# Self-attention followed by a pooled non-local block: the matrix engine's work spread evenly, the DMAs' partial row sums merged by the vector engine, and a new order of loads where the second layer starts

## The chip, the cores and the metric

The kernel runs on one core of a Trainium2 chip. The metric is the device time of one execution in microseconds (us), as a median over runs. The engines are called by the names of the profile: PE is the matrix engine (PEld its weight loads), ACT the scalar engine, DVE the vector engine, POOL the general-purpose engine, which issues one of the two DMA queues, and SP the engine that only issues DMAs. Sixteen DMA engines carry the transfers of both queues.

## The reference, cut to what matters

`x` is 2 x 256 x 64 x 64 in float32, so each of two batches has 256 channels at n = 4096 places. Layer 0 is self-attention with 8 heads of 32 channels; layer 1 is a non-local block with 1024 pooled keys.

```python
# layer 0
qkv = einsum('oc,bchw->bohw', w_qkv, x); q, k, v = split(qkv, 3)      # 8 heads, d = 32
attn = softmax(einsum('bhdi,bhdj->bhij', q, k) / sqrt(d), axis=-1)    # 4096 x 4096 for each head
out = einsum('bhij,bhdj->bhdi', attn, v)
x = einsum('oc,bchw->bohw', w_proj, out.reshape(b, c, h, w)) + x
# layer 1
theta = conv1x1(x[:, :64]); phi = maxpool2(conv1x1(x[:, 64:])); g = maxpool2(conv1x1(x))
y = softmax(theta^T phi, axis=-1) @ g
x = batchnorm(conv1x1(y)) + x
```

## The kernel before

**Stages.** Each batch passes through five stages: projection and attention of head group 0 (four heads), projection and attention of head group 1, and the second layer. The attention stages are most of the time. Each engine has one program, written out by hand in the order in which it is to work, and waits on semaphores.

**One attention stage.** The queries are cut into NC = 8 chunks of CH = 512, the keys into JT = 32 tiles of 128. One key tile of one chunk has four heads, which makes four "units" of 128 keys x 512 queries. ACT turns three units at a time into exponentials (line 595), from one of two PSUM banks of three units, into a ring of 36 units (nine key tiles) in SBUF. Such a group of three is a "step"; a stage has 342 steps, a chunk has 42 2/3. At step k PE waits for the exponentials of step k, computes the scores of step k + 2 (line 513, 12 matmuls in float16) and then some of the product with the values (`values`, line 526, float32). The product is counted in "halves": four matmuls, one for each head, on 256 of the 512 queries of a key tile. `halves_by(k)` says how many halves are done by the end of step k: 1.5 on average, at most two behind what is ready.

**Row sums.** The softmax's denominators are sums over keys. The key tiles of a chunk are added up elementwise: those in `SUM_V` by DVE into `acc` (line 648), those in `SUM_D` (eight) by POOL's accumulating DMAs into `accD`, two DMAs for each tile (k = 0, 1; lines 674 and 677), each waiting for the one before it of its own k. Then PE multiplies with a matrix of ones: `sums_of_acc` (line 489) five steps into the next chunk, `sums_of_dma` (line 497) nine steps into it. DVE copies the chunk's output out of PSUM (`output_out`, line 605) in the middle of the chunk's last add, which it splits in two for that, and the sums (`sums_out`, line 613) before the add of key tile 11 of the next chunk; the reciprocal (line 651) follows the add of tile 21. The last chunk of a stage is summed after the stage (`tensor_end`, lines 485 to 497).

**Slots.** Before ACT writes a key tile into the ring, `slot_free` waits until the tile nine before it has been used: by the values, and by DVE's add or by both accumulating DMAs.

**From attention to the second layer.** Unnormalised outputs went to DRAM (`o_dram`), inverse sums too (`r_dram`). When the last scores are out, SP issues (`rows_ahead`, line 1296) the projection's weights, the outputs of chunks 1 to 3 (`output_in`, line 1288) and then the inverse sums of chunks 0 to 6 as rows (line 1303). PE spreads the rows over the partitions with a small matmul (`broadcast`, line 838) for chunks 0, 1, 2 and 7; for chunks 3 to 6 (`BY_DMA`) SP's DMAs do it (`spread_rows`, line 1239, two DMAs of 256 KB each). DVE multiplies (`normalise`, line 1092), PE projects (line 848). In `sync` SP issues all eight spreading DMAs, then the outputs of chunks 4 to 7, then stores the last chunk's inverse sums (line 1260), waits for that to land, and loads them as rows (line 1247), which `broadcast(7)` needs.

Of the kernel before, what the change touches and what calls it, by code (L numbers as in the profile page):

```python
# [18 lines left out]
G = 4  # L19
# [22 lines left out]
SUM_D = [2, 6, 9, 13, 16, 20, 23, 27]  # L42
# [21 lines left out]
def halves_by(k):  # L64

    if k == GROUPS - 1:
        return 2 * NC * JT
    halves = min(k * GROUP // 2, 2 * (min((k + 1) * GROUP, UNITS) // G))
    return halves - (halves % (2 * JT) in (1, 2 * JT - 1))
# [20 lines left out]
def conv_seq(nc, x, wqkv, wproj, gw, tw, pw, ww, vectors, biases, out, r_dram, r1_dram):  # L90
# [3 lines left out]
    with ExitStack() as root:  # L94
# [351 lines left out]
        def attention(g, ready_for, ahead):  # L446
# [7 lines left out]
            s_sum = sem(root, f"s_sum_{g}")  # L454
            s_o_free = sem(root, f"s_o_free_{g}")
# [22 lines left out]
            def sums_of_acc(pe, c):  # L478
                if c < NC - 1:
                    pe.wait_ge(s_o_free, c + 1)  # L480
                else:
                    pe.wait_ge(s_l_free, c)
                    r = (NC * JT - 1) * G % RING
                    for h in range(G):
                        nc.tensor.matmul(sums_in(c)[h * D:(h + 1) * D, :], ones[:], P[:, r + h, :],
                                         start=True, stop=False)
                pe.wait_ge(s_add, adds_by(c))
# [5 lines left out]
            def sums_of_dma(pe, c):  # L493
                for k in range(2):
                    pe.wait_ge(s_dma[k], 16 * len(SUM_D) * (c + 1))
                for h in range(G):
                    last = nc.tensor.matmul(sums_in(c)[h * D:(h + 1) * D, :], ones[:], accD[c % 2][:, h, :],
                                            start=False, stop=True)
                last.then_inc(s_sum, 1)

            def tensor(pe, free):
# [38 lines left out]
                for k in range(GROUPS):  # L540
# [25 lines left out]
            def tensor_end(pe):  # L566
                sums_of_acc(pe, NC - 1)
                sums_of_dma(pe, NC - 1)
# [37 lines left out]

            def sums_out(dve, c):
                dve.wait_ge(s_sum, (c + 1) * 2)
                if c:
                    dve.wait_ge(s_out, 16 * c)  # L610
                elif ahead:
                    dve.wait_ge(ahead.signals["out"], 16 * NC)
                nc.vector.tensor_copy(L[:], sums_in(c)).then_inc(s_l_free, 1)

            def vector(dve, at, room):
# [9 lines left out]
                for c in range(NC):  # L625
                    for n in range(ADDS):
                        if n == 7 and c:
                            sums_out(dve, c - 1)
# [13 lines left out]
                        if j == JT - 1:  # L642
                            nc.vector.tensor_tensor(new[:, 0:2, :], old[:, 0:2, :], P[:, r:r + 2, :], ALU.add)
                            output_out(dve, c)
                            nc.vector.tensor_tensor(new[:, 2:G, :], old[:, 2:G, :], P[:, r + 2:r + G, :], ALU.add
                                                    ).then_inc(s_add, 1)
                        else:
                            nc.vector.tensor_tensor(new, old, P[:, r:r + G, :], ALU.add).then_inc(s_add, 1)  # L648
                        if n == 14 and c:
                            dve.wait_ge(s_out, 16 * c)  # L650
                            nc.vector.reciprocal(Ls[:, g, c - 1:c, :], Ls[:, g, c - 1:c, :]).then_inc(s_inv, 1)
# [4 lines left out]
            def gpsimd(pool, clean):  # L656
                for c in range(NC):
# [3 lines left out]
                    for i, j in enumerate(SUM_D):  # L661
                        for k in range(2):
# [4 lines left out]
                            if i == 0:  # L667
                                if c:
                                    pool.wait_ge(s_dma[k], 16 * len(SUM_D) * c)
                                if c >= 2:  # L670
                                    pool.wait_ge(s_sum, (c - 1) * 2)
                                elif ahead:
                                    pool.wait_ge(ahead.signals["sum"], (NC - 1 + c) * 2)
# [30 lines left out]
            sems = [s_ready, s_exp, s_pv, s_add, s_sum, s_o_free, s_l_free, s_out, s_inv, s_r, s_b, s_tr, s_ost] + s_dma + s_q  # L704
# [3 lines left out]
        def second_layer(behind, homes):  # L708
# [98 lines left out]
            def gpsimd(pool, b, clean):  # L807
                if b is not None:
                    pool.wait_ge(behind.signals["sum"], NC * 2)
# [432 lines left out]
            def sync(sp, b, dram, following):  # L1242
# [388 lines left out]
```

## Time and profile before

| | |
|---|---|
| median of 3 runs | 2556.77 us (2555.61 to 2557.37) |
| the profiled execution | 2555.43 us, of which the span of its instructions is 2553.8 us |
| PE busy | 2461.8 us (96%) |
| ACT busy | 2220.2 us (87%) |
| DVE busy | 2144.3 us (84%) |
| POOL's DMA queue, share of the 16 DMA engines' time | 52.7% |

The profile is one execution, its times counted from the first instruction. A busy share is an average over stages with different limits, and matmuls are pipelined, so that PE is shown busy where it isn't at its peak; idle time before an instruction, and what ended it, tells more. The attention stages are at about 44 to 514, 552 to 1023, 1310 to 1780 and 1816 to 2287 us.

### The profile page before, as it was taken

The page shows a single profiled execution, that of the slowest core. Times are in us where ns is not written, and L with a number is a line of the kernel's source. Part 1 is how long each engine was busy: PE and PEld are TensorE (multiplying, and loading weights), DVE is VectorE, ACT ScalarE, POOL GpSimd, SP SyncE. Part 2 cuts the span into 40 slices and gives each one's busy share as a digit, 9 for nine tenths or more (in the row PEclk, how much of TensorE's full clock was granted, in tenths as well). Part 3 has the DMA queues.
Part 4 walks back from the last instruction along what each step waited for, and adds up shares of the span by engine and source line. Part 5 has one row for each costly group of instructions (what it writes and reads, how often), then busy time and mean ns, then how long its engine had stood idle before and what let it go on. Part 6 is the DMA issues. An engine that isn't in the chain of part 4 may idle for free.

```text
span 2553.8 us, 74568 instructions
## 1 busy us (share of the span) xinstructions
PE 2461.8 (96%) x33252; PEld 1076.2 (42%) x33256; DVE 2144.3 (84%) x1382; ACT 2220.2 (87%) x1826; POOL 455.7 (18%) x652
## 2 busy tenths in 40 slices
PE   8999999999999999699999999999999999987998
PEld 4444444444444444244454444444444444433443
DVE  6999999979999999596579999998799999976954
ACT  7999999989999999266489999998999999983663
POOL 0222222202222222010002222222122222220100
PEclk9999999999999999899999999999999999998999
DMA  8777777767777777401277787776777777682011
GB/s 240 161 156 154 160 156 159 151 177 160 158 155 155 159 160 155 114 1 71 82 200 160 157 161 155 157 148 142 198 157 156 160 156 158 144 176 71 1 58 43
DMA packets 150227, 360.14 MB, mean 141 GB/s; under 512 B 23072, under 2 KB 65376, under 8 KB 149632
## 3 DMA queue, kind: packets, MB, share of 16 engines
q0 software_dynamic: 73728, 268.47, 52.7%
q1 hardware_dynamic: 76176, 86.92, 11.2%
q8 instruction: 258, 4.23, 0.7%
q14 instruction: 65, 0.53, 0.1%
HBM read 52.76 MB, written 33.85 MB: 34 GB/s over the span
## 4 chain that ended last, share of the span: by engine, by line
PE 34%; ACT 29%; issue 16%; DMA 13%; DVE 6%; SPq 1%; ACTq 0%; POOL 0%; POOLq 0%; DVEq 0%
ACT arena L595 27%; DMA arena<-arena 11%; PE scores L513 8%; PE psOL L526 7%; PE psOL L952 6%; DVE arena L648 3%; PE scores L334 3%; PE psOL L875 1%; DMA arena<-att_out 1%; PE scores L345 1%; SPq L1239 1%; PE scores L939 1%; PE scores L940 1%; PE scores L929 1%; PE scores L930 1%
## 5 line engine op out<-in xcount | busy, mean ns | idle before, releaser
L595 ACT ACTIVATE arena<-scores 128x1536 f32<-128x1536 f32 x1368 | 1847.8, 1534 | 33.3 <-PE scores L513 29.9
L648 DVE TENSOR_TENSOR arena<-arena 128x2048 f32<-128x2048 f32 x704 | 1613.2, 2292 | 141.1 <-ACT arena L595 89.3
L513 PE MATMUL scores<-arena 96*32 96x512 f16 x16384 | 1128.1, 380 | 11.7 <-ACT arena L595 10.7
L526 PE MATMUL psOL<-arena 128*32 128x256 f32 (+1 forms) x13312 | 1117.1, 428 | 1.3 <-ACT arena L595 1.3
L513 PEld LDWEIGHTS scores<-arena 96*32 96x32 f16 x16384 | 382.5, 95 | 702.8 <-ACT arena L595 404.7
L677 POOL DMA_DIRECT2D arena<-arena x448 | 388.0, 895 | 1150.8 <-ACT arena L595 911.7
L526 PEld LDWEIGHTS psOL<-arena 128*32 128x32 f32 x13312 | 399.3, 110 | 370.7 <-issue 43.3
L952 PE MATMUL psOL<-arena 128*128 128x512 f16 x768 | 170.3, 379 | 0.0
L674 POOL DMA_DIRECT2D arena<-arena x64 | 35.2, 554 | 570.6 <-ACT arena L595 570.3
L1216 DVE SCALAR_TENSOR_TENSOR arena<-arena 128x1536 f16<-128x1536 f32 (+1 forms) x48 | 75.9, 1581 | 65.1 <-ACT arena L1062 63.3
L1055 ACT ACTIVATE arena<-scores 128x1536 f32<-128x1536 f32 (+1 forms) x48 | 62.5, 1301 | 72.0 <-PE scores L940 72.0
L952 PEld LDWEIGHTS psOL<-arena 128*128 128x128 f16 x768 | 75.1, 98 | 90.6
L992 ACT ACTIVATE arena<-X 128x512 f16<-128x512 f32 x32 | 20.2, 630 | 105.7 <-DVE X L1098 105.7
L1034 ACT ACTIVATE arena<-scores,arena 128x1024 f32<-128x1024 f32 x64 | 71.1, 1112 | 26.9 <-POOL arena L819 25.6
L334 PE MATMUL scores<-arena,wq_hi 128*128 128x512 f16 x256 | 72.3, 385 | 10.5 <-DVE wq_lo L263 8.6
L1202 DVE TENSOR_REDUCE arena<-scores 128x1 f32<-128x1024 f32 x64 | 78.0, 1221 | 5.0 <-PE scores L930 3.0
L376 ACT ACTIVATE arena<-scores 128x1024 f16<-128x1024 f32 x32 | 32.7, 1021 | 40.9 <-PE scores L334 40.0
L1062 ACT ACTIVATE arena<-arena 128x1536 f16<-128x1536 f32 (+1 forms) x48 | 64.4, 1341 | 2.8
L397 DVE SCALAR_TENSOR_TENSOR arena<-X,arena 128x1024 f16<-128x1024 f32 x32 | 39.1, 1223 | 27.8 <-ACT arena L363 27.8
L848 PE MATMUL scores<-arena 128*128 128x512 f32 x128 | 61.1, 622 | 0.0
L939 PE MATMUL scores<-arena 128*128 (+1 forms) x128 | 48.5, 379 | 6.1 <-ACT arena L1055 5.7
L929 PE MATMUL scores<-arena 128*128 128x512 f16 x128 | 48.7, 381 | 5.5 <-ACT arena L1034 5.4
(120 smaller groups left out, 1240.7 us busy)
## 6 DMA issues: line engine op xcount, KB each, us to landing
arena<-arena POOLq DMA_DIRECT2D x512, 512.0 KB, 5.3
arena<-qk_parts SPq DMA_DIRECT2D x192, 128.0 KB, 3.8
qk_parts<-arena SPq DMA_DIRECT2D x32, 512.0 KB, 3.7
X<-in_x SPq DMA_DIRECT2D x16, 512.0 KB, 5.1
att_out<-arena SPq DMA_DIRECT2D x32, 256.0 KB, 2.1
arena<-att_out SPq DMA_DIRECT2D x16, 512.0 KB, 12.2
out<-arena SPq DMA_DIRECT2D x32, 256.0 KB, 2.0
arena<-att_inv SPq DMA_DIRECT2D x16, 256.0 KB
```

Of the source, the lines that this page charges most:

```text
L334: last = nc.tensor.matmul(slot(w), wq[wp][:, t, outs], xp[:, t, c * CH:(c + 1) * CH], start=(n == 0 and t == 0), stop=(n == 2 and t == CT ...
L513: last = nc.tensor.matmul(bank[k % 2][m * D:(m + 1) * D, i * CH:(i + 1) * CH], KS[0:3 * D, h, j * 128 + m * D:j * 128 + (m + 1) * D], QS2[ ...
L526: last = nc.tensor.matmul(both(c)[h * D:(h + 1) * D, lo:hi], V[:, j, h * D:(h + 1) * D], P[:, r + h, lo:hi], start=(j == 0), stop=(j == JT ...
L595: nc.scalar.activation(P[:, u % RING:u % RING + size, :], bank[k % 2][:, 0:size * CH].rearrange("p (u n) -> p u n", n=CH), ACT.Exp, scale= ...
L648: nc.vector.tensor_tensor(new, old, P[:, r:r + G, :], ALU.add).then_inc(s_add, 1)
L677: nc.gpsimd.dma_start(dst, src, accum_op=ALU.add).then_inc(s_dma[k], 16)
L929: nc.tensor.matmul(two_banks(i)[:, ks], TA[:, its], PA[:, ks], start=True, stop=False)
L939: nc.tensor.matmul(dst, PA[:, m], TA[:, bass.ds(c * CH, CH)], start=True, stop=False)
L952: last = nc.tensor.matmul(psOL[:, t * CH:(t + 1) * CH], w[:, m, ts], v[:, p, m, :], start=(n == 0), stop=(n == 3 * MT - 1))
L1034: nc.scalar.activation(junk[:, i % 2, :], two_banks(i), ACT.Exp, bias=stat[:, 0, i:i + 1], scale=SCORE1, accum_out=l1[:, i:i + 1]).then_in ...
L1202: nc.vector.tensor_reduce(mx[:, i:i + 1], two_banks(i), AX.X, ALU.max).then_inc(s_mx, 1)
L1216: nc.vector.scalar_tensor_tensor(out=Pl[:, p, ms, :], in0=P32[:, p, ms, :], scalar=PS, in1=Ph[:, p, ms, :], op0=ALU.mult, op1=ALU.subtract ...
```

## The change

Five things are changed.

1. `SUM_D` has nine key tiles, mostly three apart, and `SUM_V` 23 instead of 24.
2. DVE adds `accD` to `acc` itself (`merge`), before its add of key tile 10 of the next chunk; PE has one product with ones for each chunk (`sums_of_both`), 18 steps into the next chunk, instead of two. The last chunk of a stage is summed as before.
3. `halves_by_step` replaces `halves_by`: halves are done at an even rate of 68 x 3 / 128 = 1.594 a step, start at step 6, and pause for four halves at the step with the product with ones. They trail what is ready by up to eight halves at the start and six or seven later.
4. DVE's last add of a chunk isn't split any more; `output_out` comes before its add of key tile 3 of the next chunk, `sums_out` before that of tile 19, the reciprocal after that of tile 25.
5. `rows_ahead` loads the rows of inverse sums first, then the weights and the outputs of chunks 1 and 2 only. In `sync` each chunk's two spreading DMAs are followed by that chunk's output (chunks 3 to 6), and chunk 7's output comes last.

```diff
-SUM_D = [2, 6, 9, 13, 16, 20, 23, 27]
+SUM_D = [2, 5, 8, 12, 15, 18, 21, 24, 27]
...
-    halves = min(k * GROUP // 2, 2 * (min((k + 1) * GROUP, UNITS) // G))
-    return halves - (halves % (2 * JT) in (1, 2 * JT - 1))
+SUMS, BEHIND = 18, 2
+SUM_STEPS = [exps_through(c, JT - 1) + SUMS for c in range(NC - 1)]
+def halves_by_step():
+    rate = (2 * JT + 4) * GROUP / (G * JT)
+    first = exps_through(0, JT - 1) + SUMS
+    start = first - (first * GROUP / 2 - BEHIND) / rate
+    done, at = [], 0
+    for k in range(GROUPS):
+        ready = 2 * (min((k + 1) * GROUP, UNITS) // G)
+        share = int(rate * (k + 1 - start)) - 4 * sum(1 for n in SUM_STEPS if n <= k)
+        to = ready if k == GROUPS - 1 else min(ready, share)
+        to -= to % (2 * JT) in (1, 2 * JT - 1)
+        at = max(at, to)
+        done.append(at)
+    return done
...
-            def sums_of_acc(pe, c):
+            def sums_of_both(pe, c):
+                pe.wait_ge(s_o_free, c + 1)
+                pe.wait_ge(s_merged, c + 1)
                 for h in range(G):
-                    last = nc.tensor.matmul(sums_in(c)[h * D:(h + 1) * D, :], ones[:], acc[c % 2][:, h, :],
-                                            start=(c < NC - 1), stop=False)
+                    last = nc.tensor.matmul(both(c)[h * D:(h + 1) * D, :], ones[:], acc[c % 2][:, h, :],
+                                            start=True, stop=True)
                 last.then_inc(s_sum, 1)
...
                     for c in range(NC - 1):
-                        if k == exps_through(c, JT - 1) + 5:
-                            sums_of_acc(pe, c)
-                        if k == exps_through(c, JT - 1) + 9:
-                            sums_of_dma(pe, c)
-                    at, end = halves_by(k - 1) if k else 0, halves_by(k)
+                        if k == exps_through(c, JT - 1) + SUMS:
+                            sums_of_both(pe, c)
+                    at, end = HALVES[k - 1] if k else 0, HALVES[k]
...
+            def merge(dve, c):
+                for k in range(2):
+                    dve.wait_ge(s_dma[k], 16 * len(SUM_D) * (c + 1))
+                dve.wait_ge(s_add, adds_by(c))
+                nc.vector.tensor_tensor(acc[c % 2], acc[c % 2], accD[c % 2], ALU.add).then_inc(s_merged, 1)
...
-                        if n == 7 and c:
+                        if n == 1 and c:
+                            output_out(dve, c - 1)
+                        if n == 6 and c:
+                            merge(dve, c - 1)
+                        if n == 12 and c:
                             sums_out(dve, c - 1)
...
                                 if c >= 2:
-                                    pool.wait_ge(s_sum, (c - 1) * 2)
+                                    pool.wait_ge(s_merged, c - 1)
...
                 for n in BUFFERS:
                     spread_rows(sp, dram, n)
+                    c = BY_DMA[n]
+                    if c >= 4:
+                        sp.wait_ge(s_oin[c % 4], 16)
+                    output_in(sp, c)
                 if b is not None:
                     sp.wait_ge(behind.signals["ost"], 16 * NC)
-                for c in range(4, NC):
-                    sp.wait_ge(s_oin[c % 4], 16)
-                    output_in(sp, c)
+                sp.wait_ge(s_oin[(NC - 1) % 4], 16)
+                output_in(sp, NC - 1)
...
             def rows_ahead(sp, dram):
-                sp.dma_start(wp_sb, wproj.rearrange("(t p) o -> p t o", p=128)).then_inc(s_wp, 16)
-                for c in range(1, 4):
-                    output_in(sp, c)
                 for k in range(2):
                     cs = slice(ROWS[k] * CH, ROWS[k + 1] * CH)
                     for g in range(NG):
                         sp.dma_start(Rr[32 * g:32 * g + G, cs], r_dram[dram, g * G:(g + 1) * G, cs]).then_inc(s_rc[k], 16)
+                sp.dma_start(wp_sb, wproj.rearrange("(t p) o -> p t o", p=128)).then_inc(s_wp, 16)
+                for c in range(1, 3):
+                    output_in(sp, c)
```

## Rows read from the trace of the kernel before

**Rows 1.** lines of instructions, costliest first: busy, mean ns of one | idle before them and what ended it

```profile
L595 ACT ACTIVATE arena<-scores 128x1536 f32<-128x1536 f32 x1368 | 1847.8, 1534 | 33.3 <-PE scores L513 29.9
L648 DVE TENSOR_TENSOR arena<-arena 128x2048 f32<-128x2048 f32 x704 | 1613.2, 2292 | 141.1 <-ACT arena L595 89.3 <-DVE arena L648 1.4
```

**Rows 2.** ACT in order of time, two stretches between its idle times: start, length, what

```profile
114.13 5.48 ACT L595 ACTIVATE arena<-scores 128x1536 f32<-128x1536 f32 x4 [0.62 <-PE scores L513]
120.22 52.69 ACT L595 ACTIVATE arena<-scores 128x1536 f32<-128x1536 f32 x39 [0.62 <-PE scores L513]
```

**Rows 3.** who waited for whom over the whole span: total us, times, longest

```profile
ACT arena L595 <- PE scores L513: 29.9, 68, 0.6
...
POOL arena L677 <- DMA arena<-arena: 237.2, 117, 5.6
...
DVE arena L1092 <- DMA arena<-att_out: 25.3, 2, 12.7
...
PE scores L838 <- DMA arena<-att_inv: 15.8, 2, 8.4
```

**Rows 4.** PE in order of time around one product with ones, 170 to 173 us

```profile
170.50 0.82 PE L513 MATMUL scores<-arena 96*32 96x512 f16 x12
171.15 1.04 PE L489 MATMUL psOL<-arena,ones 128*32 128x512 f32 x8
172.01 0.61 PE L526 MATMUL psOL<-arena 128*32 128x256 f32 x8
172.44 0.83 PE L513 MATMUL scores<-arena 96*32 96x512 f16 x12
```

**Rows 5.** PE in order of time: a stage's end, and two `broadcast` of the second layer

```profile
513.95 1.92 PE L526 MATMUL psOL<-arena 128*32 128x512 f32 x16 [0.34 <-ACT arena L595]
...
1031.78 2.08 PE L838 MATMUL scores<-arena,spread 4*128 4x512 f32 x4 [7.36 <-DMA arena<-att_inv]
...
1085.97 1.13 PE L838 MATMUL psOL<-arena,spread 4*128 4x512 f32 x4
```

**Rows 6.** DMAs of 60 to 500 us: share of 16 engines' time; issues, KB each, us to landing

```profile
q0 software_dynamic: 17442, 63.52, 72.7%
...
arena<-arena POOLq DMA_DIRECT2D x121, 512.0 KB, 5.3
...
att_out<-arena SPq DMA_DIRECT2D x7, 256.0 KB, 2.1
```

**Rows 7.** POOL in order of time: two issues of one chain (k = 1)

```profile
190.17 0.86 POOL L677 DMA_DIRECT2D arena<-arena  x1 [1.31 <-DMA arena<-arena]
...
197.16 0.87 POOL L677 DMA_DIRECT2D arena<-arena  x1 [2.92 <-ACT arena L595]
```

**Rows 8.** one piece of the chain that ended last, at the second layer's start

```profile
1054.31 16.30 DMA arena<-att_out
```

**Rows 9.** SP's DMA issues in order of time, second layer's start

```profile
1021.77 0.39 SPq L1297 DMA_DIRECT2D arena<-in_w_proj  x1
...
1040.75 13.12 SPq L1239 DMA_DIRECT2D arena<-att_inv  x8
...
1062.85 5.77 SPq L1260 DMA_DIRECT2D att_inv<-Ls  x2
1075.38 0.63 SPq L1247 DMA_DIRECT2D arena<-att_inv  x2
```

**Rows 10.** DVE in order of time: `normalise` of chunk 3, and of chunk 4

```profile
1052.44 1.21 DVE L1092 TENSOR_TENSOR arena<-arena 128x1024 f32<-128x1024 f32 x1
...
1070.63 1.23 DVE L1092 TENSOR_TENSOR arena<-arena 128x1024 f32<-128x1024 f32 x1 [12.70 <-DMA arena<-att_out]
```

**Rows 11.** windows: us, length, busy of the engines, granted clock, DMA share, GB/s

```profile
1042.00:1056.00 14.00, 14.00 (x41) 5.72 (x40) 10.78 (x17) 4.92 (x8) 0.70 (x1) 1.00 0.26 89
1058.00:1066.00 8.00, 1.22 (x3) 0.19 (x1) 0.00 (x0) 0.83 (x2) 0.00 (x0) 0.88 1.04 239
1066.00:1074.00 8.00, 1.48 (x4) 0.58 (x5) 3.27 (x5) 0.63 (x1) 0.00 (x0) 0.50 0.30 99
```

More of the change, by code:

```diff
@@ L61, in adds_through @@
     return max(1, sum(1 for t in SUM_V if t <= j) - 1)
-def halves_by(k):
-    if k == GROUPS - 1:
-        return 2 * NC * JT
-    halves = min(k * GROUP // 2, 2 * (min((k + 1) * GROUP, UNITS) // G))
-    return halves - (halves % (2 * JT) in (1, 2 * JT - 1))
+SUMS, BEHIND = 18, 2
[13 more added lines that the diff above has]
+    return done
+HALVES = halves_by_step()
 BY_DMA = [3, 4, 5, 6]
@@ L454, in attention @@
             s_sum = sem(root, f"s_sum_{g}")
+            s_merged = sem(root, f"s_merged_{g}")
             s_o_free = sem(root, f"s_o_free_{g}")
@@ L476, in adds_by, with sums_of_last @@
                 return (c + 1) * ADDS - (c == NC - 1)
-            def sums_of_acc(pe, c):
[L479 to L487, printed above, removed]
+            def sums_of_both(pe, c):
+                pe.wait_ge(s_o_free, c + 1)
+                pe.wait_ge(s_merged, c + 1)
                 for h in range(G):
-                    last = nc.tensor.matmul(sums_in(c)[h * D:(h + 1) * D, :], ones[:], acc[c % 2][:, h, :],
-                                            start=(c < NC - 1), stop=False)
+                    last = nc.tensor.matmul(both(c)[h * D:(h + 1) * D, :], ones[:], acc[c % 2][:, h, :],
+                                            start=True, stop=True)
                 last.then_inc(s_sum, 1)
-            def sums_of_dma(pe, c):
+            def sums_of_last(pe):
+                pe.wait_ge(s_l_free, NC - 1)
+                r = (NC * JT - 1) * G % RING
+                for h in range(G):
+                    nc.tensor.matmul(psO[h * D:(h + 1) * D, :], ones[:], P[:, r + h, :], start=True, stop=False)
+                pe.wait_ge(s_add, adds_by(NC - 1))
+                for h in range(G):
+                    nc.tensor.matmul(psO[h * D:(h + 1) * D, :], ones[:], acc[(NC - 1) % 2][:, h, :],
+                                     start=False, stop=False)
                 for k in range(2):
-                    pe.wait_ge(s_dma[k], 16 * len(SUM_D) * (c + 1))
+                    pe.wait_ge(s_dma[k], 16 * len(SUM_D) * NC)
                 for h in range(G):
-                    last = nc.tensor.matmul(sums_in(c)[h * D:(h + 1) * D, :], ones[:], accD[c % 2][:, h, :],
+                    last = nc.tensor.matmul(psO[h * D:(h + 1) * D, :], ones[:], accD[(NC - 1) % 2][:, h, :],
                                             start=False, stop=True)
@@ L566, in tensor_end @@
             def tensor_end(pe):
-                sums_of_acc(pe, NC - 1)
-                sums_of_dma(pe, NC - 1)
+                sums_of_last(pe)
             def slot_free(act, m):
@@ L641, in vector @@
                             old = new
[L642 to L649, printed above, removed]
+                        nc.vector.tensor_tensor(new, old, P[:, r:r + G, :], ALU.add).then_inc(s_add, 1)
+                        if n == 16 and c:
                             dve.wait_ge(s_out, 16 * c)
@@ L670, in gpsimd @@
                                 if c >= 2:
-                                    pool.wait_ge(s_sum, (c - 1) * 2)
+                                    pool.wait_ge(s_merged, c - 1)
                                 elif ahead:
-                                    pool.wait_ge(ahead.signals["sum"], (NC - 1 + c) * 2)
+                                    pool.wait_ge(ahead.signals["sum"], NC - 1 + c)
                                 nc.gpsimd.dma_start(dst, src).then_inc(s_dma[k], 16)
@@ L808, in gpsimd @@
                 if b is not None:
-                    pool.wait_ge(behind.signals["sum"], NC * 2)
+                    pool.wait_ge(behind.signals["sum"], NC)
                 nc.gpsimd.memset(TB[CM:128, :].bitcast(F32), 0.0).then_inc(s_pad, 1)
```

4 lines of the change are left out of this document (2 added, 2 removed).

## The prediction

> **What bounds the kernel now.** I read the lines by cost first. ACT's exponentials keep it busy for 1847.8 us and it stands idle before them for only 33.3 us, 29.9 of it for PE's scores [rows 1, 3]. 39 of them take 52.69 us, so a step takes ACT 1.351 us [rows 2], and 342 steps of four stages 1848 us. That is a floor the change doesn't touch. So the attention stages can give at most those 33 us. Then PE in order of time. Where it never waits for ACT, the scores of a step take 0.65 us (170.50 to 171.15), one product with ones 0.86 (to 172.01), one half 0.43 (to 172.44); two halves are four matmuls of the product's shape, so 0.86 [rows 4]. A step costs PE 0.65 + 1.5 x 0.43 = 1.30 us on average, 0.05 less than ACT's. A chunk has 42.7 steps and so 2.2 us to spare, of which the two products take 1.7. PE may fall behind by the 0.70 us that the scores leave of a step before ACT waits; a product in a step of two halves makes 0.65 + 3 x 0.43 + 0.43 = 2.37 us, 1.02 behind at once, and four steps later only 0.2 has been made good when the second product comes. That is the pair of 0.62 us waits in rows 2, 68 waits in all [rows 3]. Last the waits of the rest: at the start of the second layer PE waits 15.8 us in two batches for the rows of inverse sums and DVE 25.3 us for an output from DRAM [rows 3].
>
> **PE in the attention stages.** One product with ones fewer a chunk saves 0.86 us of PE. With 1.594 halves a step PE needs 0.65 + 1.594 x 0.43 = 1.34 us, just under 1.351. The step with the product has no halves (0.65 + 0.86 = 1.51 us, 0.16 behind), and the next has none either (0.65 us): everything is made good there. Two steps of two halves in a row leave it 2 x 0.16 behind. Nothing comes near 0.70. I take 1.5 us of the 29.9 as left: **-28.4 us** (bounds: all 33.3; or half of it, if the 0.01 us of margin isn't there).
>
> **The end of a stage.** Before, PE does four halves after the last but one exponentials (1.92 us in the row) [rows 5]. Now the last step has five and the one before it one, six instead of four, 0.86 us more, and the last five wait for the last exponentials: I take 1.0. At the end of a group 0 stage the next projection's first waits pass through PE, so +1.0 for each of two stages. At a group 1 stage's end it is in the sum below.
>
> **DVE.** Before, 22 adds and a split one; now 22 adds and the merge, all of 128 x 2048 at 2.29 us [rows 1]: 52.7 us plus two copies and a reciprocal, in 57.6. The cost is nothing. `output_out` waits for key tile 31's values. By the new list they are done in steps 44, 87, 130, 172, 215, 258 and 301, counted from 0, and DVE comes to it after tile 1's add, which begins when 46, 88, 131, 174, 216, 259 and 302 steps of exponentials are done and takes 1.7 steps: the values are there just before it. The merge waits for the DMAs of tile 27, whose exponentials are 14 tiles (25 us) old; behind it on DVE stand the adds, and behind those ACT's slots. `sums_out` comes at tile 18, the product at tile 13 to 14. SP's store of sums, its wait for the reciprocal and the store of that move from tile 21 to 25 with DVE; the loads of queries behind them wait for the chunk's last scores anyway. Values trail by at most four of the ring's nine tiles, and a slot is due only eight tiles (14.4 us) after it was filled.
>
> **The accumulating DMAs.** 121 of them hold 72.7% of 440 us of the sixteen engines [rows 6]: 2.64 us each, 5.3 for a key tile. Three tiles of ACT's time are 5.4 us. From tile 12 to 27 the DMAs now run with nothing to spare, and no tile is skipped. The nearest row for a tile behind another: k = 1 was issued at 190.17 and 197.16, 7.0 us apart over three tiles [rows 7]; POOL already waits 237.2 us for landings [rows 3]. With two in flight half a turn apart the bound is 5.3 us, in step with each other it is 7.0. I take 5.9, since the further both trail the more they alternate: lateness grows 0.5 us a tile, about 3 us from tile 12 to 27 on top of 2 to 4. Landing takes 5.3 us, so tile 27 is free some 11 us after its exponentials, and due at 14.4. A chunk needs 9 x 5.9 = 53 of 57.6 us. So nothing, but if that cover goes, ACT waits. After a group 0 stage PE's last product needs tile 27's second DMA, which I count 0.5 us late: +0.5 for each of two.
>
> **The second layer's start.** PE stood still for 7.36 us before 1031.78, so it had ended at 1024.4 [rows 5]. Now it ends at 1025.4. The first rows are SP's first issues after 1021.77 [rows 9] and small; two issues at 0.4 us and the 2.1 us that a store takes to land [rows 6] make 1024.7, so PE goes straight on, and at full clock: `broadcast` took 2.08 us at 1031.78 and 1.13 at 1085.97 [rows 5]. SP's first spreading DMA follows after 1.1 (broadcast) + 1.3 (six filler matmuls) + 2.6 (twelve with ones) + 0.7 + 0.6 (DVE's copy, SP's store), plus 0.7 for the last accumulating DMA: 1032.4 instead of 1040.75 [rows 9], 8.4 earlier. The output of chunk 0, which SP can fetch only after the reciprocal's store, is about 7 us later than before and has its load's time until 1027; PE's project needs it at 1033.
>
> Next stop: chunk 4's output was issued at 1054.31, landed 16.3 us later [rows 8] and cost DVE 12.7 [rows 10]. Why so long? While SP's eight spreading DMAs ran, the sixteen engines were busy 0.26 of the time at 89 GB/s: four engines carry them. Once the outputs are queued it is 1.04 at 239, and at the end again 0.30 at 99 [rows 11]. Outputs use all sixteen, so their quarter on the four waits behind all the spreading. With chunk by chunk order, chunk 3 needs two spreads and an output: 2 x 262 KB at 89 GB/s and 131 KB at 99 make 7.2 us, with the slowing while all sixteen work about 8. From 1034 on that serves chunks 3 to 6 at 1042, 1050, 1058, 1066; DVE wants them at 1044, 1050, 1056, 1062 (6.0 us a chunk, and from 1052.44 less 8.4). The 12.7 us wait goes, 2 us at a time come back.
>
> What is late next is chunk 7's rows. Their store is queued behind everything; SP issued the load at 1075.38 to 1076.0 [rows 9], landing at 1078.1, and `broadcast(7)` came at 1085.97, with 7.9 us to spare. The queue starts 8.4 us earlier but holds one output more (1.3 us on the four engines, 1.0 of slowing): rows at 1072.0. PE could be there at 1085.97 - 8.4 - 12.7 = 1064.9. So it stands for 7 us there and the gain is 1085.97 - 1072.0 = 14.0 us, not 21.1; 0.5 is lost to the lower clock after standing. In batch 1 PE waited 8.4 us instead of 7.4, so 1.0 more. Together **-28.0 us** (bounds: -21 each if the rows come in time; -8 each if only the first wait goes).
>
> The Trainium skill (DMA: Bandwidth & Descriptors, Rules for kernel authors) says that an outermost dimension below 16 confines a DMA to as many engines, here the four heads; the share of 0.26 agrees. It puts an engine at about 27 GiB/s (Specifications), 116 GB/s for four where rows 11 show 89. By that the eight spreads would take 18 us, not 23.6, chunk 7's rows would come 5.5 us earlier and the sum would be 2491.
>
> **Sum.** 2555.4 (span 2553.8) - 28.4 + 2.0 + 1.0 - 28.0 = 2502.0 for an execution like the profiled one, whose time lies 1.3 below the median: I say 2502.
>
> **Rivals.** (a) Chunk 7's rows come in time, 14 us more: 2488, chance 0.13. For it: queued work may flow faster interleaved; against: the store is last in a queue that bound before. (b) PE's even rate leaves no real margin, its waits only spread out, 14 us less: 2516, 0.12. For it: 1.34 against 1.351 rests on hundredths in rows 4; against: the gaps of rows 2 come in pairs at the products only, so PE does keep up between them. (c) The accumulating DMAs run late past 14.4 us near tiles 24 to 27, one us a chunk, 28 us lost: 2530, 0.12. That is 6.5 us for each tile of the nine. For it rows 7; against: seven tiles of pause after tile 27. (d) Slower: at 7.0 us for each of nine tiles a chunk takes 63 us, 5.4 over ACT's 57.6, in 28 chunks and more +150: 2650. It decides from 6.6 us a tile on, where 9 x 6.6 is 1.8 over and 28 times that has used up the gain. For it: 7.0 is what rows 7 show over three tiles; against: k = 0 was not late then, and 5.3 us is all that two DMAs need. Chance 0.05. (e) It does nothing, because another wait stands behind each: 2556, 0.03. Forecast, 2502 with its own range 2492 to 2511: 0.55.
>
> A measurement of this kernel tells about 0.2% (5 us) from nothing. Range: from (a) to half way into (c), 2485 to 2522, leaving out 0.18. Faster 0.92, same 0.03, slower 0.05.
>
> **What would show it.** Right: ACT idle before line 595 for PE near zero in waits a few hundredths long; 1.6 us more of PE after the last exponentials; no PE wait at the first `broadcast`; no 12.7 us wait of `normalise`; a new PE wait of 5 to 8 us at `broadcast(7)`. Wrong: ACT idle before line 595 with the DMAs as releaser, POOL's issues at tiles 24 and 27 over 6 us behind their exponentials, or PE's steps at 1.36 us and more.

## The result, and the profile after

The changed kernel takes 2525.49 us (median of 4, 2520.97 to 2527.07) against 2556.19 for the one before on the same chip: ratio 0.9876 [0.9862, 0.9889], 31 us faster. The forecast was 2502, its range 2485 to 2522. The direction was right; 23.5 us of the 54 us that were forecast are missing. The profiled execution has a span of 2525.1 us, 28.7 less than before.

Two of the costliest lines of the kernel after (busy, mean ns | idle before, releaser):

```profile
L609 ACT ACTIVATE arena<-scores 128x1536 f32<-128x1536 f32 x1368 | 1848.6, 1465 | 16.0 <-PE scores L530 11.0
L666 DVE TENSOR_TENSOR arena<-arena 128x2048 f32<-128x2048 f32 x700 | 1601.9, 2291 | 146.1 <-ACT arena L609 104.0
```

ACT's exponentials cost the same as in [rows 1]; the idle time before them fell from 33.3 to 16.0 us, not to the 4.9 forecast. The 28 merges (line 625) take DVE 64.0 us, without idle time before them.

Its waits (who for whom: total us, times, longest):

```profile
POOL arena L695 <- DMA arena<-arena: 504.8, 220, 4.8
...
PEld scores L856 <- DMA arena<-in_w_proj: 8.1, 1, 8.1
PE scores L856 <- issue: 7.6, 1, 7.6
...
ACT arena L609 <- PE scores L530: 11.0, 20, 2.1
...
DVE arena L1110 <- DMA arena<-att_out: 6.9, 5, 2.0
...
DVE arena L1234 <- DMA arena<-pool_inv: 6.1, 2, 4.0
...
ACT arena L609 <- DMA arena<-arena: 3.3, 4, 1.4
```

Against [rows 3]: ACT's 68 waits for PE are now 20, some of them 2 us long where 0.6 was the longest. The output's 25.3 us became 6.9. But the first `broadcast` of the second layer (line 856) still waits some 7.5 us in each batch. It had waited for the rows of inverse sums. Its releaser is now the weights, `in_w_proj`, in batch 1; in batch 0 the view says "issue" for PE and the weights for PE's weight load (PEld). And POOL waits twice as long for landings (504.8 for 237.2).

ACT in order of time, the first attention stage (a line stands for a run without idle time):

```profile
45.14 8.15 ACT L609 ACTIVATE arena<-scores 128x1536 f32<-128x1536 f32 x6
53.52 1.45 ACT L609 ACTIVATE arena<-scores 128x1536 f32<-128x1536 f32 x1 [0.23 <-PE scores L530]
55.23 2.79 ACT L609 ACTIVATE arena<-scores 128x1536 f32<-128x1536 f32 x2 [0.26 <-PE scores L530]
59.71 54.28 ACT L609 ACTIVATE arena<-scores 128x1536 f32<-128x1536 f32 x40 [1.70 <-PE scores L530]
114.16 55.48 ACT L609 ACTIVATE arena<-scores 128x1536 f32<-128x1536 f32 x41 [0.16 <-PE scores L530]
171.08 117.88 ACT L609 ACTIVATE arena<-scores 128x1536 f32<-128x1536 f32 x87 [1.44 <-DMA arena<-arena]
```

The pairs of 0.62 us [rows 2] are gone, and two waits are new: 2.2 us within ten steps of the start (1.0, 2.3 and 0.2 in the other stages), and some of 0.2 to 1.6 us late in a chunk's turn, of which the view names the DMAs for part (3.3 us in four waits, where all of them make 6.1). The stages (from the first exponentials to the end of the last), 470.1 to 470.2 us before, take 467.6, 464.6, 466.6 and 465.5: 16.4 us less in all, not 28.4.

PE at that start, and the windows of 4 us there (length, busy of PE, PEld, DVE, ACT, POOL, granted clock, DMA share, GB/s):

```profile
46.63 0.83 PE L530 MATMUL scores<-arena 96*32 96x512 f16 x12 [0.54 <-ACT arena L609]
47.97 0.83 PE L530 MATMUL scores<-arena 96*32 96x512 f16 x12 [0.51 <-ACT arena L609]
...
49.31 0.83 PE L530 MATMUL scores<-arena 96*32 96x512 f16 x12 [0.19 <-ACT arena L609]
50.65 0.83 PE L530 MATMUL scores<-arena 96*32 96x512 f16 x12 [0.51 <-ACT arena L609]
52.00 1.47 PE L530 MATMUL scores<-arena 96*32 96x512 f16 x12 [0.51 <-ACT arena L609]
...
53.70 2.79 PE L530 MATMUL scores<-arena 96*32 96x512 f16 x24
```

```profile
46.00:50.00 4.00, 2.77 (x41) 0.78 (x37) 3.02 (x7) 4.00 (x4) 0.00 (x0) 1.00 0.85 243
50.00:54.00 4.00, 2.98 (x33) 0.74 (x33) 0.24 (x2) 3.77 (x4) 1.28 (x2) 0.75 0.68 227
54.00:58.00 4.00, 4.00 (x36) 1.02 (x32) 3.90 (x3) 3.74 (x3) 1.02 (x2) 0.50 0.26 103
```

The new list gives PE almost nothing but scores for the first steps: 0.83 us of work, then mostly some 0.5 of waiting. In this stage the granted clock then falls from 1.00 to 0.50 (2.4 to 1.2 GHz), 12 matmuls take 1.47 us, and ACT waits. In the kernel before every window here shows 1.00.

SP's issues and PE, both at the second layer's start:

```profile
1015.46 2.73 SPq L1321 DMA_DIRECT2D arena<-att_inv  x4
1018.24 0.40 SPq L1322 DMA_DIRECT2D arena<-in_w_proj  x1
1018.68 2.77 SPq L1309 DMA_DIRECT2D arena<-att_out  x2
...
1035.62 1.15 SPq L1257 DMA_DIRECT2D arena<-att_inv  x2
1036.81 0.48 SPq L1309 DMA_DIRECT2D arena<-att_out  x1
...
1038.60 3.37 SPq L1309 DMA_DIRECT2D arena<-att_out  x1
...
1069.71 0.63 SPq L1265 DMA_DIRECT2D arena<-att_inv  x2
```

```profile
1015.24 3.79 PE L543 MATMUL psOL<-arena 128*32 128x512 f32 x40
1026.63 2.08 PE L856 MATMUL scores<-arena,spread 4*128 4x512 f32 x4 [7.59 <-issue]
```

The rows now go out first, the weights behind them. PE ends at 1019.0 and starts again at 1026.63, 8.4 us after the weights' issue. From the end of the exponentials to `broadcast(7)` it was 63.0 and 64.9 us in the two batches and is 55.0 and 55.2: 17.7 us less, forecast 28. `broadcast(7)` waits 0.66 us in batch 0 and not at all in batch 1, where 7 were forecast.

The sum of what is read: -16.4 (stages), +1.8 (from a group 0 stage's end to the next, 38.32 to 39.24 twice), -17.7. That is -32.3, and a wait of DVE for `pool_inv` 4.3 us longer (6.1 for 1.8; from 2.2 to 6.0 in the kernels below, so it varies) makes it -28.0 of the 28.7.

### The profile page after: what moved, and what is told of

Its sections match the earlier page's. It is cut to its first block, busy times and chain, and to the rows that moved or that the text cites. A ratio compares the mean times of both kernels' runs of the same rounds, so it can differ in the third digit from the quotient of the medians.

```text
span 2525.1 us, 73776 instructions
## 1 busy us (share of the span) xinstructions
PE 2433.7 (96%) x32808; PEld 1073.7 (43%) x32808; DVE 2127.0 (84%) x1350; ACT 2221.0 (88%) x1826; POOL 511.0 (20%) x716
## 4 chain that ended last, share of the span: by engine, by line
PE 38%; ACT 34%; DMA 13%; issue 9%; DVE 4%; SPq 2%; ACTq 0%; POOL 0%; POOLq 0%; DVEq 0%
ACT arena L609 32%; DMA arena<-arena 12%; PE scores L530 10%; PE psOL L543 9%; PE psOL L970 7%; PE scores L349 3%; DVE arena L666 2%; PE psOL L893 1%; PE scores L360 1%; PE scores L957 1%; PE scores L958 1%; SPq L1257 1%; PE scores L947 1%; PE scores L948 1%; PE scores L866 1%
## 5 line engine op out<-in xcount | busy, mean ns | idle before, releaser
L666 DVE TENSOR_TENSOR arena<-arena 128x2048 f32<-128x2048 f32 x700 | 1601.9, 2291 | 146.1 <-ACT arena L609 104.0
L543 PE MATMUL psOL<-arena 128*32 128x256 f32 (+1 forms) x13088 | 1105.7, 434 | 0.0
L530 PEld LDWEIGHTS scores<-arena 96*32 96x32 f16 x16384 | 394.6, 95 | 720.0 <-ACT arena L609 423.7
L695 POOL DMA_DIRECT2D arena<-arena x512 | 443.1, 884 | 1192.9 <-ACT arena L609 673.1
L543 PEld LDWEIGHTS psOL<-arena 128*32 128x32 f32 x13088 | 390.8, 110 | 349.0 <-issue 15.9
L692 POOL DMA_DIRECT2D arena<-arena x64 | 35.3, 553 | 464.2 <-ACT arena L609 405.1
L625 DVE TENSOR_TENSOR arena<-arena 128x2048 f32<-128x2048 f32 x28 | 64.0, 2284 | 0.0
```

Of the source, the lines that this page charges most:

```text
L530: last = nc.tensor.matmul(bank[k % 2][m * D:(m + 1) * D, i * CH:(i + 1) * CH], KS[0:3 * D, h, j * 128 + m * D:j * 128 + (m + 1) * D], QS2[ ...
L543: last = nc.tensor.matmul(both(c)[h * D:(h + 1) * D, lo:hi], V[:, j, h * D:(h + 1) * D], P[:, r + h, lo:hi], start=(j == 0), stop=(j == JT ...
L695: nc.gpsimd.dma_start(dst, src, accum_op=ALU.add).then_inc(s_dma[k], 16)
```

## The experiments

Each was timed in three rounds beside the kernel before on the same chip (its medians 2558.04, 2557.46 and 2556.43 in three groups). "Wait of the weights" is PE's `pe.wait_ge(s_wp, 16)`, which in both kernels stands ahead of `broadcast(0)`, though only the projections behind it use the weights. Where two edited kernels are compared below, it is by their medians, and some of these come from different groups. By the ratios to the kernel before, the moved wait is worth 17 us on the changed kernel, the early halves 7, eight tiles 10 and the weights first 6.

**The order alone.** The kernel before, with SP's new order of loads only (abridged):

```diff
+                for k in range(2):                       # rows_ahead: rows first
+                    ... Rr ... r_dram ...
                 sp.dma_start(wp_sb, ...).then_inc(s_wp, 16)
-                for c in range(1, 4):
+                for c in range(1, 3):
                     output_in(sp, c)
                 for n in BUFFERS:                        # sync: output behind each spread
                     spread_rows(sp, dram, n)
+                    output_in(sp, BY_DMA[n])
```

> The kernel before with the new order of SP's loads alone (part 5 of the change). Theory W (weights): PE's first broadcast is held by the projection's weights, which now come after the rows, so its wait of 7 to 8 us stays and only DVE's 12.7 us wait goes: 8 us a batch, about 2540. Rival R (rows): the rows did come in time and the part gives what I forecast for it, 28 us: about 2528. If the times of both halves of the change add up, this and the next run must together give the whole 31 us.

2533.8, ratio 0.9904 [0.9888, 0.9921]. The order gives 24 us by itself. Its stages are the old ones (470.2 to 470.5). PE at its second layer's start:

```profile
1030.35 2.08 PE L838 MATMUL scores<-arena,spread 4*128 4x512 f32 x4 [5.50 <-issue]
```

5.50 us, and 5.75 with `in_w_proj` as releaser in batch 1, where the forecast has none. The time lies between the two that were expected: the wait of the weights is there, and yet the order gives more than the 8 us a batch of theory W (10.3 and 12.7 from the exponentials' end to `broadcast(7)`).

**The order undone.** The changed kernel with the old order.

> The changed kernel with the old order of SP's loads (parts 1 to 4 alone). My forecast for these parts was -25 us (2531). The trace of the changed kernel shows stages of attention only 2.4 to 5.6 us shorter each, 16 in all: then about 2540. Theory S+D (start and DMA): the missing 9 to 12 us are ACT's idle times at the stages' starts (5.6 us) and near the chunks' ends behind late accumulating DMAs (6 us); they should be there in this run too, as neither has to do with the second layer.

2548.64, ratio 0.9962 [0.9949, 0.9976]: 9 us for all the rest together, where about 16 were expected. The stages fall by 21.8 us in sum (463.1 to 466.5), but PE's wait for the rows grows from 7.4 and 8.4 [rows 3, 5] to 9.94 and 11.06, and from the exponentials' end to `broadcast(7)` it is 6.2 us more in the two batches. The stage ends take 1.8 more and the wait for `pool_inv` 4.0 (5.8 for 1.8), which leaves 9.8 of the 21.8. DVE's 24.6 us for outputs is back. That the ninth tile's late DMAs hold back the rows isn't tested in this kernel. Below, with eight tiles, PE's first wait in the second layer is 5.53 and 6.08 us for 7.59 and 7.19.

**The wait of the weights moved.** The changed kernel, and:

```diff
-                pe.wait_ge(s_wp, 16)
                 if between:
                     pe.wait_ge(behind.signals["exp"], GROUPS)
                 broadcast(0)
...
                     keep_busy(slot(0), 4)
+                pe.wait_ge(s_wp, 16)
                 for c in range(NC):
```

> The changed kernel with PE's wait for the projection's weights moved from before the first broadcast to before the first projection. Theory W: PE goes into the first broadcast within 1 us of the stage's end instead of 7.6 us after it, at full clock, and the run is 12 to 16 us faster than the changed kernel (2510 to 2514), less what chunk 7's rows and the spreading DMAs then hold back (so 2517 at worst). Rival: PE waits there for the rows or the last exponentials: no change, 2525.

2506.91, ratio 0.9809 [0.9782, 0.9837]: 18.6 us below the change. (Three runs took 2504.94 to 2507.13 us and one 2518.66, hence the wide interval.) PE in order of time:

```profile
1012.78 3.79 PE L543 MATMUL psOL<-arena 128*32 128x512 f32 x40
1018.73 1.13 PE L856 MATMUL scores<-arena,spread 4*128 4x512 f32 x4 [2.16 <-DMA arena<-att_inv]
...
1062.97 1.13 PE L856 MATMUL psOL<-arena,spread 4*128 4x512 f32 x4 [0.78 <-DMA arena<-att_inv]
```

The wait falls to 2.16 and 1.77 us, its releaser is the rows again, and `broadcast` takes 1.13 us: full clock, as forecast. From the exponentials' end to `broadcast(7)` it is 48.8 and 47.2 us, 14 less than in the changed kernel for both together. The rival, that PE waits there for something else, is out.

**The order and the moved wait, on the kernel before.**

> The kernel before with the new order of SP's loads and the weights' wait after the first broadcast: part 5 of the change as I had costed it. My forecast for it was 28 us; the trace of the changed kernel with the wait moved shows 14 to 17 us from the last exponentials to chunk 7's broadcast in each batch. So 30 to 34 us faster than before, about 2525. Rival: without the late accumulating DMAs of the ninth tile the rows come later relative to PE and 24 us stay what they were with the order alone: 2534.

2522.44, ratio 0.9875 [0.9858, 0.9891], 34 us. Stages 470.0 to 470.2; the exponentials' end to `broadcast(7)` 45.6 and 44.9 us, against 63.0 and 64.9. PE there:

```profile
1025.58 1.13 PE L838 MATMUL scores<-arena,spread 4*128 4x512 f32 x4 [1.62 <-DMA arena<-att_inv]
...
1068.10 1.13 PE L838 MATMUL psOL<-arena,spread 4*128 4x512 f32 x4 [0.74 <-DMA arena<-att_inv]
```

So with the overlooked wait out of the way the new order is worth 34 us by the medians and 32 by the ratio, 7 to 10 more than without (24), and more than the 28 that were costed.

**The weights first.** The changed kernel with SP's issues in the order weights, rows, outputs.

> The changed kernel with the weights' DMA issued first, then the rows, then the outputs of chunks 1 and 2. Theory W, second form: what held the weights was their place behind the rows and before 1 MB of outputs in a queue that the last accumulating DMAs share. If the place matters, PE's first broadcast comes 3 to 6 us earlier a batch and the run is 6 to 12 us faster than the changed kernel. Rival: rows and weights land together in any order and only the wait's place in PE's program counts: within 3 us of the changed kernel.

2517.33, ratio 0.9853 [0.9837, 0.987], 8 us below the change. PE now waits 4.23 and 2.57 us, for the rows. DMAs of the changed kernel from 1012 to 1030 us (issues, KB each, median us to landing) show why a place in this queue costs so much:

```profile
arena<-att_out SPq DMA_DIRECT2D x3, 512.0 KB, 9.1
arena<-arena POOLq DMA_DIRECT2D x2, 512.0 KB, 8.6
arena<-in_w_proj SPq DMA_DIRECT2D x1, 256.0 KB, 8.2
att_out<-arena SPq DMA_DIRECT2D x1, 256.0 KB, 8.2
```

The store in the last line is of the kind that [rows 6] have at 2.1 us in mid-stage; here it takes 8.2. The last accumulating DMAs and three outputs are under way beside it. The trace of the kernel before has the same at this place (its DMAs of 1010 to 1080 us), so the 2.1 us were read from the wrong stretch:

```profile
arena<-in_w_proj SPq DMA_DIRECT2D x1, 256.0 KB, 6.3
att_out<-arena SPq DMA_DIRECT2D x1, 256.0 KB, 8.4
```

**The halves from the start.** The changed kernel, and in the list of halves:

```diff
+        if k < SUM_STEPS[0]:
+            share = k * GROUP // 2
```

> The changed kernel with the values' halves of each stage's first 61 steps at the old rate (from step 2 on, 1.5 a step, at most two behind) and the new list after that. Theory S: PE's granted clock falls to its half at about the eighth step because it has only scores to do until step 6, and ACT then waits 0.2 to 2.3 us a stage (5.6 us in four stages). With work from step 2 on the clock stays at 1.0 and the time falls by 4 to 6 us, to about 2520. Rival: the waits come from the three halves at once in step 6 and the 0.01 us of margin; then ACT's idle times move but stay, and the time is the same within 1 us.

2519.93, ratio 0.985 [0.9834, 0.9867], 5.6 below the change. ACT's waits for PE are 11, together 2.7 us, the longest 0.4; the stages take 463.9, 465.3, 464.0 and 463.1, 8.0 us less. The windows at the first stage's start:

```profile
46.00:50.00 4.00, 3.30 (x49) 1.05 (x45) 2.21 (x6) 4.00 (x4) 0.01 (x1) 1.00 0.79 219
50.00:54.00 4.00, 4.00 (x69) 1.71 (x65) 1.52 (x2) 3.81 (x3) 1.28 (x2) 1.00 0.71 265
```

The clock stays at 1.00. The waits for the DMAs stay too (5.1 us in 6).

With the late list the clock doesn't always fall. The kernel with the order undone has the same program in its stages as the changed kernel, and its first stage shows (length, busy of PE, granted clock, DMA share, GB/s)

```profile
50.00:54.00 4.00, 2.67 (x41) 1.00 0.64 234
```

and 0.19 us of waiting at that start; the changed kernel's own fourth stage has 1.00 and 0.19 us too. So it isn't the three halves of step 6 that cost (the rival), but the slow clock.

This also says how much a difference of stages between two traces is worth. Over the four traces whose stages have the same program (the change, order undone, moved wait, weights first) their sum is 1864.3, 1858.9, 1861.9 and 1862.6 us, in the mean 1861.9. Against that mean the early halves save 5.7 us, not 8.0, which fits the 5.6 of the time. The waits at the four starts are 5.6, 2.3, 3.9 and 2.8 us in these traces, 3.6 in the mean, and 0.8 with early halves; what the rest of the 5.7 is isn't settled.

**The old list of halves.** The changed kernel with the levelling taken back, one product with ones a chunk.

> The changed kernel with the old list of halves (1.5 a step, at most two behind, no pause at the product), so that only the merge and the one product with ones remain of the change on PE. Theory: the halves' even rate is needed, since the product of 0.86 us in a step with one or two halves still leaves PE more than 0.70 us behind: ACT waits 0.3 to 0.6 us at most of 28 products, 10 to 15 us in all instead of the 11 us of the changed kernel, but the waits at the stages' starts are gone; 2522 to 2530. Rival: one product a chunk alone brings it all, since two products close together were the trouble; then ACT's waits for scores fall below 4 us and the time to 2518 or less.

2522.45, ratio 0.9864 [0.9848, 0.9881]. The stages take 1864.0 us in sum, those of the changed kernel 1864.3. 39 waits for PE of at most 0.6 us (16.3 us in all) are left of 68. The time is at the edge of what the theory expected, and the rival (below 4 us of waits) is out: one product fewer doesn't end the waits. But it gave all the gain of the stages that the change has; the levelling, as built, took about as much at the starts as it brought later, and pays only with the early halves (1856.2 us).

**Eight DMA tiles.** The changed kernel with the old `SUM_D = [2, 6, 9, 13, 16, 20, 23, 27]`.

> The changed kernel with eight key tiles for the accumulating DMAs again, and nothing else. Theory D as in the run with both repairs: 5 to 9 us faster than the changed kernel (2517 to 2520), ACT's waits with the DMAs as releaser gone, the waits at the stages' starts still there.

2515.61, ratio 0.9835 [0.9819, 0.9852], 10 below the change. ACT never waits for the DMAs; POOL's waits for landings fall from 504.8 to 305.6 us, the stages to 464.7, 463.2, 464.4 and 463.2 (8.8 less than the changed kernel's, 6.4 less than the mean of the four traces). The waits at the starts stay (1.77 us in the first stage), which leaves two separate causes. How the ninth tile is late shows on POOL in the changed kernel, in order of time:

```profile
161.22 0.87 POOL L695 DMA_DIRECT2D arena<-arena  x1 [3.88 <-DMA arena<-arena]
163.03 0.87 POOL L695 DMA_DIRECT2D arena<-arena  x1 [0.94 <-ACT arena L609]
```

These are the two DMAs of key tile 27 of chunk 1, the last of the nine. (Both halves of a tile, k = 0 and 1, are issued on line 695, 677 in the kernel before; line 692, 674 before, is the plain copy with which a chunk starts.) Its exponentials end 80 steps after 45.14: steps 78 and 79 from 153.4 to 156.1 (29 steps of 1.353 after 114.16). ACT was due to take that slot again at 169.6, 13.5 us after them, and takes it at 171.08, 1.44 us late: 15.0 us after the exponentials and 8 after the second issue.

**Moved wait and early halves.**

> The changed kernel with both repairs, the weights' wait after the first broadcast and the values' halves from step 2 on. If the two losses are separate, as theories W and S have them, their gains add: 19 us and 5.5 us below the changed kernel, about 2501. Rival: they share a cause (the state of PE's clock) and the second adds less than 2 us: 2505 or more.

2501.23, ratio 0.9779 [0.9763, 0.9796]. The two gains add up, and with both the changed kernel is at the forecast's time. In part that is luck: its stages give 23.7 us where 28.4 were forecast, and the starts of the second layer 34.4 where it was 28.0.

**And eight tiles.**

> The run before it with eight key tiles for the accumulating DMAs again (2, 6, 9, 13, 16, 20, 23, 27), the merge by DVE kept. Theory D: the ninth tile makes the DMAs late; ACT's waits with the DMAs as releaser (5 us) go, and the rows of inverse sums land 1 to 2 us earlier a batch: 6 to 9 us faster than the run before it, about 2494. Rival V: the ninth tile pays for the merge. With eight, DVE has 23 adds and a merge of 2.29 us, two copies and a reciprocal, 56.6 us in a chunk of 57.6; it falls behind after the merge, the slots come free late, and ACT waits for adds: no gain or some us slower, 2500 to 2510.

2494.78, ratio 0.9753 [0.9736, 0.9769]. Stages of 462.5 to 462.8 us, 0.70 of it idle; ACT in the first one:

```profile
44.94 6.81 ACT L611 ACTIVATE arena<-scores 128x1536 f32<-128x1536 f32 x5
51.94 232.55 ACT L611 ACTIVATE arena<-scores 128x1536 f32<-128x1536 f32 x172 [0.20 <-PE scores L532]
```

This is the floor that the prediction named. DVE's 732 adds (1674.5 us) and 28 merges (64.0 us) lie beside it, and ACT never waits for DVE, so rival V, that DVE needs the ninth tile's relief, is out.

**And a shorter tail.** In the list of halves, `if k >= GROUPS - 3: share = at + 3`, so that values don't pile up behind the last exponentials.

> The run before it with three halves in each of the last steps but one of a stage, so that two instead of five are left after the last exponentials. By my step of 1.0 us a stage: 1 us less at each of four stage ends, 2 to 4 us faster than the run before it. Rival: at the end DVE's adds and the last accumulating DMA set the time, nothing changes.

2493.29, ratio 0.9744 [0.9727, 0.976], the fastest here: 32 us below the changed kernel and 64 below the one before. The exponentials' end to `broadcast(7)` is 46.05 and 45.9 us, after 47.6 and 48.5. By medians alone the 1.5 us are within what this measurement tells from nothing, and the wait for `pool_inv` is 1.8 us shorter in this trace, so the gain isn't shown.

**Chunk 6's inverse sums by PE too,** on top of that, for earlier rows of chunk 7.

> The fastest version so far (both repairs, eight tiles, three halves before the end) with chunk 6's inverse sums spread by PE instead of two of the eight spreading DMAs. My step on the second layer's start says that the four engines under the spreading DMAs set its pace: 3.3 us each. DVE's waits for outputs (3 us a batch) and the wait for chunk 7's rows (0.5 us) should nearly go; PE's extra 1.1 us lies beside DVE. 4 to 7 us faster in two batches, about 2487. Rival: DVE's own 6.0 us a chunk or the outputs' loads set the pace; then 0 to 2 us.

2500.16 (2493.29 to 2503.38), ratio 0.9771 [0.9755, 0.9787]: 7 slower by the medians of two groups, where 4 to 7 faster were expected. The intervals of the two ratios just touch, so it is clear that nothing was gained, less clear how much was lost. PE no longer waits for chunk 7's rows, yet comes later. The windows of this kernel, and under them those of the one without:

```profile
1046.00:1050.00 4.00, 1.55 (x4) 0.57 (x5) 3.34 (x5) 0.63 (x1) 0.00 (x0) 0.82 0.19 58
1050.00:1054.00 4.00, 4.00 (x8) 1.16 (x7) 2.83 (x5) 3.36 (x6) 0.00 (x0) 0.50 0.26 70
1054.00:1058.00 4.00, 4.00 (x6) 1.69 (x5) 2.16 (x4) 0.59 (x2) 0.00 (x0) 0.50 0.01 2
```

```profile
1046.00:1050.00 4.00, 3.67 (x10) 1.38 (x8) 2.33 (x5) 3.14 (x7) 0.00 (x0) 1.00 0.26 98
1050.00:1054.00 4.00, 1.78 (x6) 0.51 (x6) 3.84 (x6) 1.09 (x2) 0.00 (x0) 0.87 0.14 29
1054.00:1058.00 4.00, 3.79 (x6) 1.34 (x7) 3.73 (x7) 2.35 (x4) 0.00 (x0) 0.50 0.20 58
```

PE had stood for 3.30 us behind DVE's wait for chunk 5's output, the clock fell to 0.50, and `broadcast(6)` (2.08 us) and the projection after it (8 matmuls in 6.57 us, where 3.70 at full clock) ran at half speed. Without the edit PE stands twice (2.63 and 2.28 us) and the clock falls too, but later, and less work falls into the slow stretch. That the clock is the whole of the 7 us is read from the trace, not tested by itself.

## Why the prediction was wrong

**The step that failed** is in the second layer's start: "two issues at 0.4 us and the 2.1 us that a store takes to land make 1024.7, so PE goes straight on". The step looks only at the rows. PE's program waits for the weights ahead of `broadcast(0)`, in the kernel before as well, where they were SP's first issue and never the last to come. The change puts them behind the rows, and the wait is as long as ever with another releaser (7.59 and 7.19 us, forecast none). Moving it on the changed kernel gave 18.6 us by the medians and 17 by the ratios; on the kernel before with the new order 7 to 11, which brings that part past its forecast of 28. The landing was mis-sized besides: even with the wait moved, rows issued at 1013.00 let PE go at 1018.73, 5.7 us later and not 2.9, so PE stands for 2 us. The 2.1 us were a store's in mid-stage; at this very place a store took 8.4 us in the kernel before.

**The second start term, broadcast(7), was mis-sized.** 7 us of waiting were forecast there, 0.66 measured. In part PE was late itself by 7.6 us, but with the wait moved it is still only 0.78. The rows come earlier after the first spreading DMA than reckoned (36.0 us in both kernels, forecast 39.6), and DVE still waits for outputs (2.05 and 1.21 us before `normalise` of chunks 5 and 6 in the changed kernel), so PE arrives later. The spreading DMAs themselves start later after the exponentials (12.8 us with the wait moved, forecast 9.5); that the sum then comes out near the forecast, 48.8 us where the prediction's times make 49.1, is luck. That the 12.7 us wait goes was right. On the four engines' rate: at a share of 0.26 the windows of the last two kernels show 98, 96 (1042 to 1046 us, not printed above) and 70 GB/s, where [rows 11] show 89. The Trainium skill (DMA: Bandwidth & Descriptors, Specifications) would give an estimate of 116 at about 27 GiB/s an engine; the measurements stay below that, by 18 at the least, as the old row does.

**PE in the stages: -28.4 forecast, -16.4 measured (-18.8 in the mean of the four traces).** The arithmetic of the steady state was right: with its two side effects removed, 0.70 us of idle time a stage are left, less than the 1.2 (4.9 over four) allowed. Rival (b), PE's even rate with no margin, is refuted by that. The first side effect isn't in the prediction at all: the values' late start lets PE stand for part of each step, and at three of the changed kernel's four starts the clock falls. Early halves took 5.7 us out of the stages by the mean of the four traces; 2.8 of it are the waits at the starts, the rest lies within the 5.4 us by which these traces differ.

**The accumulating DMAs: "So nothing" was wrong, in rival (c)'s way, at a quarter to a third of its size.** Tile 27 was reckoned free 11 us after its exponentials and due at 14.4. In the rows shown above it came at 15.0 and was due at 13.5. Its second DMA was issued 6.9 us after the exponentials, 5.7 reckoned. What the reckoning lacks most is a landing of 8 us where 5.3 was the median: it added median landings where the last one of a chunk counts. The loss is 6.4 us of stages by the mean and 8.8 by the one trace (28 in (c)), over few of the 28 chunks. A cost behind the stage goes with it: PE's first wait in the second layer is 1.1 to 2.1 us shorter with eight tiles. Rival (d), 7.0 us a tile, is refuted: nine tiles fit into a chunk.

**The end of a stage** was near: +0.92 where +1.0 and +0.5 were forecast; which of the two it is wasn't tested. Merge, moved copies and `sums_out` on DVE cost nothing, as said: ACT never waits for DVE.

**The sum.** The forecast of 2502.0 was for the profiled execution, which took 2527.06 us, 25.1 more. Of these 12.0 are the stages, 10.3 the starts of the second layer and 4.3 `pool_inv`'s varying wait, less 1.2 from the stage ends; that makes 25.4. (By the median 23.5 us are missing.) The kernel with the three causes removed (the weights' wait, the late first halves, the ninth tile) stands at 2494.8, 7 below the forecast.

## What to carry to other kernels

When loads are reordered, list every wait in the consumer's program up to the instruction that is to start earlier, not only the wait that the trace names: a trace names the last to arrive, and the next one takes its place, here at nearly the same length. A list that levels an engine's work must also be read at its edges: the first steps with nothing but the short work can cost the clock. And before a difference of a few us between two traces is explained, it is worth setting it beside traces of kernels that have the same program in that stretch: here they differ by 5.4 us. A buffer's due time is missed by the latest landing, not by the median one.

## What the runs showed of the hardware

- PE's granted clock fell from 1.00 to 0.50 (2.4 to 1.2 GHz) without a long pause: over five steps (46.1 to 52.0 us) PE had worked 0.83 us or little more of every 1.35, with pauses of 0.54, 0.51, 0.19, 0.51 and 0.51 us before its work. With the same program it stayed at 1.00 in the first stage of another execution and in the fourth of this one; with halves in between it stayed at 1.00 in the first stage.
- Landings are not a constant of the transfer: accumulating DMAs of 512 KB took 5.3 us in the median of the kernel before and 8 to 8.6 in the places shown above; 256 KB took 8.2 us from issue at the second layer's start, weights and store alike, where the store took 2.1 in mid-stage.
- SP's issue of an output took 0.48 us at 1036.81, with two spreading DMAs issued before it, and 3.37 us at 1038.60, with four and an output before it (both in the changed kernel). So an issue can hold SP longer when more is queued.
